# Attention weights spread by TensorE from three 2-byte parts, and row sums of squares taken by ScalarE

## The reference

```
q = (x @ W_q + b_q)[dst];  k = (x @ W_k + b_k)[src] + e;  v = (x @ W_v + b_v)[src]
alpha = einsum('ehc,ehc->eh', q, k) / 8
ea    = exp(alpha - segment_max(alpha, dst)[dst])
attn  = ea / (segment_sum(ea, dst)[dst] + 1e-16)
out   = segment_sum((v + e) * attn[:, :, None], dst) + x @ W_skip + b_skip
x     = layernorm(x + out)            # eps 1e-5
```

## Time and profile before

| what | value |
|---|---|
| median of 3 runs | 3533.83 us |
| profiled execution | 3541.67 us |
| its span | 3539.8 us |
| mean granted TensorE clock | 0.821 |
| PE, DVE, ACT, POOL busy | 2391.4, 2366.0, 2033.0, 2122.5 us |
| DMA | 678.87 MB, mean 192 GB/s |

### The profile page before, as it was taken

The page is one execution under the profiler, slowest core; times in us unless marked ns, Lnnn a source line. Parts: engine busy times, 40 slices in busy tenths (PEclk is TensorE's granted clock), DMA queues, the critical chain, the costliest instruction groups (busy, mean ns, idle before and its releaser), DMA issues. The chain is left out here.

```text
span 3539.8 us, 54325 instructions
## 1 busy us (share of the span) xinstructions
PE 2391.4 (68%) x13252; PEld 1807.2 (51%) x13252; DVE 2366.0 (67%) x7373; ACT 2033.0 (57%) x6253; POOL 2122.5 (60%) x2026
## 2 busy tenths in 40 slices
PE   6757772599966776774577677666656657777430
PEld 4523331466645555553466566545446657776330
DVE  6669991244458869987466677699834459978442
ACT  5624441567731159997577777789834448875110
POOL 7737773277600048773677577577577767710776
PEclk9979996599978888887788788877778879987555
DMA  6735555577719954553577788789778689943231
GB/s 183 207 106 154 156 152 112 165 241 247 239 54 285 297 169 165 171 171 126 172 232 221 231 267 264 241 265 285 228 228 224 196 228 277 265 128 105 84 91 41
DMA packets 521816, 678.87 MB, mean 192 GB/s; under 512 B 98910, under 2 KB 285669, under 8 KB 521504
## 3 DMA queue, kind: packets, MB, share of 16 engines
q1 hardware_dynamic: 455202, 549.18, 50.0%
q0 software_dynamic: 65856, 125.82, 13.5%
q10 hardware_dynamic: 446, 0.40, 0.0%
HBM read 398.69 MB, written 280.39 MB: 192 GB/s over the span
## 5 line engine op out<-in xcount | busy, mean ns | idle before, releaser
L1495 POOL DMA_INDIRECT xg<-r_d,src_row x392 | 426.3, 1087 | 170.0 <-issue 115.5
L1495 POOL DMA_INDIRECT xg<-x_d,src_any x392 | 415.1, 1059 | 154.2 <-issue 116.7
L1829 POOL DMA_INDIRECT look<-table_d,ids x196 | 202.1, 1031 | 360.2 <-DVEq L1784 303.7
L2885 POOL DMA_INDIRECT out<-x_f,out_row x196 | 203.0, 1036 | 176.8 <-DVE x_f L2951 118.0
L1128 POOL DMA_INDIRECT xd<-in_x,ids x196 | 216.0, 1102 | 73.2 <-issue 51.1
L1495 POOL DMA_INDIRECT xg<-g_d,src_any x196 | 200.6, 1024 | 79.3 <-issue 52.1
L718 POOL DMA_INDIRECT rows_d<-row,slot_i x196 | 193.5, 987 | 69.5 <-issue 56.7
L2259 ACT ACTIVATE term_c<-xg,scale 128x128 f32<-128x128 f32 x392 | 125.3, 395 | 149.7 <-DMA xg<-r_d,src_row 71.4
L2611 ACT ACTIVATE term_c<-term_c,inv_deg 128x128 f32<-128x128 f32 x392 | 124.9, 392 | 130.8 <-DVE term_c L2627 130.7
L2225 PE MATMUL m_ps_c<-w_L_gnn_Wr,term_t_c 128*128 128x128 f32 x784 | 129.6, 317 | 104.2 <-ACT m_c L2250 104.2
L2171 DVE TENSOR_TENSOR_SCAN agg_t_c<-flags_c,agg_t_c,t_ps_c 128x512 f32<-128x512 bf16 x144 | 183.4, 1274 | 3.9 <-PE t_ps_c L2553 3.8
(11 more groups left out here) (510 smaller groups left out, 8407.4 us busy)
## 6 DMA issues: line engine op xcount, KB each, us to landing
flags_c<-cont_d SPq DMA_DIRECT2D x245, 128.0 KB
xm<-rows_d SPq DMA_DIRECT2D x49, 512.0 KB
m_d<-m_c SPq DMA_DIRECT2D x98, 256.0 KB, 4.4
r_d<-r_c SPq DMA_DIRECT2D x98, 256.0 KB
m_in_c<-m_d SPq DMA_DIRECT2D x98, 256.0 KB
x_c<-x_d SPq DMA_DIRECT2D x98, 256.0 KB, 4.3
e_c<-rows_d SPq DMA_DIRECT2D x98, 256.0 KB
g_d<-g_f SPq DMA_DIRECT2D x50, 258.0 KB
```

The costliest lines, as they stand in the source:

```text
L1495: pool.indirect_dma_start(out=xg[:, n % SC, k, 0:width], out_offset=None, in_=table, in_offset=bass.IndirectOffsetOnAxis(ap=rows[:, t:t + ...
L1829: pool.indirect_dma_start(out=look[:, t, :], out_offset=None, in_=table_d[:, :], in_offset=bass.IndirectOffsetOnAxis(ap=ids[:, 0, t:t + 1] ...
L2885: pool.indirect_dma_start(out=out[:, :], out_offset=bass.IndirectOffsetOnAxis(ap=out_row[:, t:t + 1], axis=0), in_=x4[:, n % SF, k, :], in ...
```

## The change

The weights are split on DVE into three 2-byte parts whose sum is the fp32 weight: a cast, the difference to it, a cast of that, and so on. Six rows (three parts of two heads) go to `attn_d`. In the weighting stage SP loads the six rows of a group onto six partitions, one DMA in place of two; PE multiplies them by a constant of ones and zeros (`heads`), which adds the three parts of a head and spreads the sum over its 64 partitions, into one of two new banks of PSUM (`w_ps`). DVE's product reads the weights there. PE makes this product for group n+1 ahead of its other work for group n.

ACT's one Square becomes four, one for each 128 columns, each with an accumulated row sum; DVE's sum over the squares goes, and its scaling reads the accumulated sums.

```diff
-        attn_d = dram("attn_d", [2, SLOTS])
+        attn_d = dram("attn_d", [6, SLOTS], BF16)
+        heads = sb("heads", [P, 2, P // 2], BF16)
...                                                   (setup, POOL)
+                pool.memset(heads[:, :, :], 1.0).then_inc(steps_g.one(), 1)
+                for base, step in ((1, 1), (3, -1)):
+                    pool.affine_select(out=heads[:, :, :], in_=heads[:, :, :], compare_op=ALU.is_gt, fill=0.0,
+                                       base=base, pattern=[[-3 * step, 2], [0, P // 2]], channel_multiplier=step).then_inc(steps_g.one(), 1)
+                    pool.wait_ge(steps_g.sem, steps_g.so_far())
...                                                   (softmax stage, SP)
-                        sp.dma_start(attn_d[v, :].rearrange("(r l) -> r l", l=LONG), seen[:, v, :]).then_inc(once_out.sem, 16)
-                    sp.wait_ge(once_out.sem, once_out.at(2))
+                        for j in range(3):
+                            sp.dma_start(attn_d[3 * v + j, :].rearrange("(r l) -> r l", l=LONG), share[:, j, v, :]).then_inc(once_out.sem, 16)
+                    sp.wait_ge(once_out.sem, once_out.at(6))
...                                                   (softmax stage, DVE, behind L1358)
+                    for j in range(3):
+                        dve.tensor_copy(share[:, j, :, :], seen[:, 0:2, :]).then_inc(steps_v.one(), 1)
+                        settled(dve)
+                        if j < 2:
+                            dve.tensor_tensor(seen[:, 0:2, :], seen[:, 0:2, :], share[:, j, :, :], ALU.subtract).then_inc(steps_v.one(), 1)
+                            settled(dve)
...                                                   (weighting stage, SP)
-                            for v in range(2):
-                                sp.dma_start(attn_b[v * 64:(v + 1) * 64, s, :], attn_d[v, n * G:(n + 1) * G].partition_broadcast(64)).then_inc(g_in[s].sem, 16)
+                            sp.dma_start(attn_6[:, s, :], attn_d[:, n * G:(n + 1) * G]).then_inc(g_in[s].sem, 16)
...                                                   (PE)
+                    def spread_shares(n):
+
+                        pe.wait_ge(g_in[n % SG].sem, g_in[n % SG].at(4 * (n // SG + 1)))
+                        if n >= 2:
+                            pe.wait_ge(weighted.sem, weighted.at(n - 1))
+                        pe.matmul(w_ps[n % 2][:, :], heads[0:6, :, :].rearrange("p a c -> p (a c)"), attn_6[:, n % SG, :], start=True, stop=True).then_inc(spread_out.sem, 1)
+
+                    spread_shares(0)
                     for n in range(GROUPS):
+                        if n + 1 < GROUPS:
+                            spread_shares(n + 1)
                         if n >= 3:
                             pe.wait_ge(x1_ready.sem, x1_ready.at(n - 2))
-                        pe.wait_ge(g_in[n % SG].sem, g_in[n % SG].at(5 * (n // SG + 1)))
...                                                   (ACT)
-                            act.activation(flat(sq[:, n % 2, :, :]), y_ps[n % 3][:, :], ACT.Square).then_inc(squared.sem, 1)
+                            for k in range(K):
+                                made = act.activation(sq[:, n % 2, k, :], y_ps[n % 3][:, chunk(k)], ACT.Square, accum_out=sums[:, n % 2, k:k + 1])
+                            made.then_inc(squared.sem, 1)
...                                                   (DVE)
-                            dve.tensor_tensor(v_in[:, s, :], v_in[:, s, :], attn_b[:, s, :], ALU.mult).then_inc(weighted.sem, 1)
+                            dve.wait_ge(spread_out.sem, spread_out.at(n + 1))
+                            dve.tensor_tensor(v_in[:, s, :], w_ps[n % 2][:, :], v_in[:, s, :], ALU.mult).then_inc(weighted.sem, 1)
...
-                            dve.tensor_reduce(ss[:, n % 2, :], sq[:, n % 2, :, :], AX.X, ALU.add).then_inc(steps_v.one(), 1)
-                            settled(dve)
-                            dve.tensor_scalar(ss[:, n % 2, :], ss[:, n % 2, :], 1.0 / D, EPS, ALU.mult, ALU.add).then_inc(spread_ready.sem, 1)
+                            dve.tensor_scalar(ss[:, n % 2, :], sums[:, n % 2, :], 1.0 / D, EPS, ALU.mult, ALU.add).then_inc(spread_ready.sem, 1)
```

More of the change, by code:

```diff
@@ L1303, in graph_kernel @@
             seen = sb("seen", [ROWS, 3, LONG], F32, st)
+            share = sb("share", [ROWS, 3, 2, LONG], BF16, st)
             weighed = signal("weighed")
@@ L1367, in _ @@
                     settled(dve)
-            for s, n in ((lined, 10), (lined_out, 9), (results, 1), (once_out, 2), (turned, 1)):
+            for s, n in ((lined, 10), (lined_out, 9), (results, 1), (once_out, 6), (turned, 1)):
                 s.spent(n)
@@ L1373, in graph_kernel @@
             v_in = sb("v_in", [P, SG, G], F32, st)
-            attn_b = sb("attn_b", [P, SG, G], F32, st)
+            attn_6 = sb("attn_6", [6, SG, G], BF16, st)
             xd_in = sb("xd_in", [P, SG, G], F32, st)
@@ L1379, in graph_kernel @@
             x1 = sb("x1", [P, 3, K, D], F32, st)
+            sums = sb("sums", [P, 2, K], F32, st)
             ss = sb("ss", [P, 2, K], F32, st)
@@ L1383, in graph_kernel @@
             x1_out = [signal(f"x1_out{s}", 16) for s in range(3)]
-            weighted, scanned, made_y, squared, spread_ready, rooted, x1_ready = (
-                signal(s) for s in ("weighted", "scanned", "made_y", "squared", "spread_ready", "rooted", "x1_ready"))
+            weighted, scanned, made_y, squared, spread_ready, rooted, x1_ready, spread_out = (
+                signal(s) for s in ("weighted", "scanned", "made_y", "squared", "spread_ready", "rooted", "x1_ready", "spread_out"))
             with ExitStack() as ps, nc.Block() as block:
                 y_ps = [bank(ps, f"y_ps{s}") for s in range(3)]
+                w_ps = [bank(ps, f"w_ps{s}") for s in range(2)]
                 @block.sync
@@ L1443, in _ @@
                             s = n % SG
-                            dve.wait_ge(g_in[s].sem, g_in[s].at(5 * (n // SG + 1)))
-                            dve.tensor_tensor(v_in[:, s, :], v_in[:, s, :], attn_b[:, s, :], ALU.mult).then_inc(weighted.sem, 1)
+                            dve.wait_ge(g_in[s].sem, g_in[s].at(4 * (n // SG + 1)))
+                            dve.wait_ge(spread_out.sem, spread_out.at(n + 1))
+                            dve.tensor_tensor(v_in[:, s, :], w_ps[n % 2][:, :], v_in[:, s, :], ALU.mult).then_inc(weighted.sem, 1)
                             if n >= 3:
@@ L1469, in _ @@
                                               inv[:, n % 2, :].unsqueeze(2).to_broadcast([P, K, D]), ALU.mult).then_inc(x1_ready.sem, 1)
-            retire([(s, GROUPS) for s in (weighted, scanned, made_y, squared, x1_ready)])
+            retire([(s, GROUPS) for s in (weighted, scanned, made_y, squared, x1_ready, spread_out)])
             for s in (spread_ready, rooted):
                 s.spent(GROUPS)
-            retire([(g_in[s], 5 * shares(s, SG)) for s in range(SG)] + [(x1_out[s], shares(s, 3)) for s in range(3)])
+            retire([(g_in[s], 4 * shares(s, SG)) for s in range(SG)] + [(x1_out[s], shares(s, 3)) for s in range(3)])
         STEPS_H, STEPS_T, STEPS_E, STEPS_F = GROUPS + 6, GROUPS + 8, GROUPS + 5, GROUPS + 11
```

## The result

The changed kernel takes 3496.81 us (median of 4 runs, 3493.4 to 3499.9) against 3535.17 (3531.9 to 3540.3) for the kernel before: a ratio of 0.9889, 95% interval 0.9873 to 0.9904, or 38 us less. The forecast was 3511 with a range of 3491 to 3529. The time lies in the range, but 2 us from the 3495 of the rival "DVE sets the pace", and the trace shows what that rival described: products 2.9 us apart and DVE's wait for the x1 store gone.

The account below looks back on a forecast made before the run. Transfers were taken to bound the weighting stage, DVE 0.1 to 0.4 us behind. 47 x (3.87 - 3.15) = -33.8, with +4 +2 +4.3 +0.8, gave -22.7 us: 3519.0 profiled, 3511 as a median, range 3491 to 3529.

Parts of the forecast that it names:

- DVE sets the pace: Rival, weighting stage: if broadcasts cost more than their bytes, the period falls to 2.9 us, giving 3495; chance 0.17.
- Term 1: Weighting stage, transfers: a group moves 0.924 MB instead of 1.18, taking 3.15 us, bounds 2.9 and 3.3.
- Term 2: Weighting stage, DVE: without the sum over squares 2.87 us a group, bounds 2.86 and 2.95; next limit, not in the sum.
- Term 3: Weighting stage, ACT: one Square becomes four with accumulators, 1.14 us, hidden with 0.5 us to spare.
- Term 4: Weighting stage, PE: 2.70 us a group at full clock; 5 of 48 groups at low clock, +4 us, bounds 0 and +14.
- Term 5: Start of the weighting stage: Bias(0) waits for group 1's loads, +2 us, bounds 0 and 3.
- Terms 6 and 7: Softmax stage's end: casts, subtractions and six stores, +4.3 us; setup: memset and two selects on POOL, +0.8 us.

Follow-up runs that it names:

- the last experiment: Changed kernel with the last product done by ScalarE, as four scaled copies, in every second group: 3496.08 us against 3532.93, ratio 0.9904 to the kernel before.

## Why the prediction was right, and where it was wrong

**What bounded the kernel** was read rightly: transfers first, DVE close behind. The sums alone gained nothing, the spread alone 7 us with DVE back to back. The two loads put back cost everything, but they brought back SyncE's issues with the bytes.

**Term 1, the transfers** (3.15 us a group, of which the sum was made) is the step that failed. The measured bound is 2.8 or less: the changed kernel moves 0.924 MB in 2.91 us, 317 GB/s, with a share of 0.92 to 0.98, and 324 GB/s were reached without the weighting product. I had divided the new bytes by the mean rate of one profiled execution, 294 GB/s, as if it were a property of the queue. Two things were wrong in that. That execution took 8 us more than the median, and the same traffic ran at up to 337 GB/s in another. And the 294 did not belong to the bytes that it divided: it is the mean of a wider window (300 between 1078 and 1260), while 1.18 MB in the measured period of 3.87 are 305 GB/s. By that, or by scaling 3.87 with the bytes (902 / 1152), the term would have been 3.03, half of the way to the 2.91 measured. The rate was not tied to the share either: the share of 1.06 counts the time that packets took, and GB/s for each unit of it was 280 to 302 in the saturated kernel before (297 / 1.06, 320 / 1.06), 304 to 318 with the sums alone, 310 with the traffic put back, 316 with the spread alone at a share of 0.81, 333 after and 334 without the weighting product at 0.97. So the time of a packet does not simply follow the load; what sets it is open. The lower bound of the term, 2.9, was right, and the rival with it had 0.17. Of that rival's two reasons one held (320 GB/s and more were kept up) and one fell (dearer broadcasts).

**Term 2, DVE:** 2.87 forecast, 2.84 and mostly 2.91 measured. It became the bound. The 3.56 that it was worked out from occurs only in the first periods; the spread-only run has 3.56 four times and then 3.63, as the changed kernel has 2.84 and then 2.91. The product that reads PSUM takes 0.68 us after, as the one that read SBUF. The 0.065 us more that the prediction estimated from the Trainium skill (VectorE: DVE Perf Modes, "The TRN2 errata") is not in the rows; the measurement decides.

**Term 3, ACT:** four squares last 1.15 us (1.14 forecast); DVE waited for them 1.1 us in 136. Right. With copies put beside them they are no longer hidden, as the last experiment shows.

**Term 4, PE:** 2.70 forecast, 2.52 in the shortest periods. The two 2-byte matmuls follow each other after 0.22 and 0.31 us:

```profile
1186.43 0.39 PE L1432 MATMUL w_ps<-attn,heads 6*128 6x512 bf16 x1
...
1186.65 0.38 PE L1440 MATMUL y_ps<-row_three,ones_b 3*128 3x512 bf16 x1
...
1186.96 1.16 PE L1442 MATMUL y_ps<-w_first,xd_in 128*128 128x128 f32 x8
```

For the clock I had put in 5 low groups and +4 us; none was low after 1086, so this term was 0 there. The low clock cost something where I had not looked for it, in the first group (term 5). The Trainium skill (TensorE: Matmul & The Clock Gate, Part 1) says that activity releases the throttle: the changed stage, with TensorE shown busy 125.5 of 136 us at 1.00, agrees, and so does the fall to 0.89 when the traffic was put back; the run without the xd product does not (last section), nor does the row at 1168 that the prediction called in agreement, where TensorE shows as busy 4.00 of 4 us at 0.50. Behind the first group the new wait for the loads of group n+1 costs nothing while the transfers are in time, and where they are not, its removal only moved the wait.

**Term 5, the start:** +2 forecast. Measured: the second product came 1.6 us earlier behind the first load, and the next two periods together took 3.2 us more than twice 2.91: +1.6. They go with TensorE's passes at 1.2 GHz, whose squares DVE waited for (3.23, above).

**Terms 6 and 7:** +4.3 and +0.8 forecast, +4.2 and +0.8 measured.

In the sum, 22.7 us were forecast between the two profiled executions and 41.9 measured. Of the 19 us between them 7 are the periods ((3.15 - 3.00) x 47), 4 the clock's term, 3.6 the stretch up to the second product (+2 forecast, -1.6 measured), and 4.6 lie in stretches without an edit. Between the medians the miss is 14 us: I had taken 7.8 us off for the long profiled execution, and that of the changed kernel lay 3.1 above its own median. That the range held is the merit of its low end, which came from the rival; the path of the forecast, transfers as the bound at 3.15, did not occur. DVE's floor stopped the gain at 2.91, and the next limit lay only 0.1 below it.

## What to carry to other kernels

When two limits lie within a few per cent, cut both or expect little: here 0 and 7 us for the halves and 38 for the whole. Before pricing a stage by its transfer rate, divide its bytes by its measured period, not by the mean of a wider window, look at how much the rate of the saturated stage varies between stretches and executions, and give the next engine's floor as the likely value if it lies inside that variation. A shorter wait in a trace is a gain only if no other engine starts to wait; compare whole periods, on one chip, side by side. And an experiment that puts transfers back also puts back the work of the engine that issues them: look at that engine's timeline before calling it traffic.

## What the runs showed of the hardware that was not expected

Without the xd product TensorE shows as busy 116.88 of 120 us and the clock is 0.50 throughout; it did not rise in the whole stage. Shown busy at 1.2 GHz is thus no sign that the clock will rise: it ran 393 matmuls in 120 us, 3.3 a microsecond, where its sibling at 1.00 ran 791 in 125, 6.3. What decides between the two levels is open; it wasn't tried further.
